# Attention stage of a four-layer kernel: division moved behind the values product, one subtraction moved to GpSimd

## What is computed

```python
ln = _ln(latents, g_l, b_l); xn = _ln(x, g_x, b_x)
q = ln @ w_q
k, v = jnp.split(jnp.concatenate([xn, ln], axis=1) @ w_kv, 2, axis=-1)
sim = jnp.einsum('bhid,bhjd->bhij', q * scale, k)       # masked keys: -max
attn = softmax(sim)
out = _ln(jnp.einsum('bhij,bhjd->bhid', attn, v) @ w_out, g_o, b_o)
x = x + jnp.tanh(g_xattn[0]) * out
```

## Time and profile before

| | us |
|---|---|
| median of 3 runs | 2226.71 |
| lowest, highest | 2226.37, 2227.58 |
| span of the profiled execution (no other time of it is recorded) | 2225.1 |
| TensorE busy in it | 2186.7 (98%) |
| weight loads | 1865.5 (84%) |
| VectorE | 1728.1 (78%) |
| ScalarE | 1282.0 (58%) |
| GpSimd | 645.1 (29%) |

### The profile page before, as it was taken

One profiled execution on the slowest core, in us unless ns is written; L12 is line 12 of the kernel. 1 busy time (PEld: TensorE's weight loads), 2 busy tenths in 40 slices (PEclk: granted clock), 3 DMA queues, 4 the chain that ended last, 5 costly groups with the idle time before them and its releaser, 6 DMA issues. The chain is left out here.

```text
span 2225.1 us, 48355 instructions
## 1 busy us (share of the span) xinstructions
PE 2186.7 (98%) x15486; PEld 1865.5 (84%) x15486; DVE 1728.1 (78%) x6112; ACT 1282.0 (58%) x3251; POOL 645.1 (29%) x1162
## 2 busy tenths in 40 slices
PE   8999999999999999999999999999999999999997
PEld 6777777777777777777699999999878888888886
DVE  6788888888888888888675555555579999999986
ACT  6776776776776776776443333433345555555553
POOL 1123223222232232232220000000355555555541
PEclk9999999999999999999899999999999999999999
DMA  5320110110110110110052222221212222222210
GB/s 189 124 97 22 37 40 23 37 39 21 40 38 20 39 39 20 40 32 27 11 161 73 81 86 72 81 77 41 89 58 65 65 65 64 65 65 65 65 39 20
DMA packets 111642, 129.57 MB, mean 58 GB/s; under 512 B 14898, under 2 KB 98089, under 8 KB 111264
## 3 DMA queue, kind: packets, MB, share of 16 engines
q1 hardware_dynamic: 98249, 105.06, 14.9%
q0 software_dynamic: 12288, 21.21, 3.3%
q10 hardware_dynamic: 855, 0.19, 0.0%
HBM read 84.26 MB, written 54.53 MB: 62 GB/s over the span
## 5 line engine op out<-in xcount | busy, mean ns | idle before, releaser
L711 ACT ACTIVATE a_prob<-a_prob,a_nmax 128x376 f32<-128x376 f32 x512 | 309.7, 606 | 155.3 <-DVE a_nmax L857 155.3
L1457 ACT ACTIVATE e_hidden<-e_first,keep_b 128x256 f32<-128x256 f32 x320 | 134.1, 471 | 283.3 <-PE e_first L80 282.8
L857 DVE CUSTOM_DVE_ANT_0 a_prob<-a_score,a_mask_row 128x376 f32<-128x376 f32 x512 | 266.6, 540 | 10.8 <-issue 5.6
L80 PE MATMUL e_second<-e_w,e_hidden 128*128 128x256 f32 x1920 | 239.5, 284 | 0.0
L80 PEld LDWEIGHTS e_second<-e_w,e_hidden 128*128 128x128 f32 x1920 | 232.6, 192 | 0.0
L869 DVE TENSOR_SCALAR a_prob<-a_prob,a_rden 128x376 f32<-128x376 f32 x512 | 220.9, 453 | 2.5
L1151 PE MATMUL a_turned<-keep_ident,a_prob 128*128 128x128 f32 (+1 forms) x1536 | 217.3, 277 | 2.8 <-DVE a_probT L876 1.6
L1151 PEld LDWEIGHTS a_turned<-keep_ident,a_prob 128*128 128x128 f32 (+1 forms) x1536 | 173.5, 142 | 43.5 <-issue 27.6
L1142 PE MATMUL a_score<-a_kT,a_qT 64*128 64x376 f32 x1024 | 196.4, 502 | 0.0
L876 DVE COPY a_probT<-a_turned 128x384 f32<-128x384 f32 x256 | 139.8, 546 | 54.4 <-PE a_turned L1151 54.4
L719 ACT ACTIVATE a_probT<-a_turned 128x384 f32<-128x384 f32 x256 | 124.9, 488 | 92.1 <-PE a_turned L1151 91.7
(11 more groups left out here) (237 smaller groups left out, 5231.1 us busy)
## 6 DMA issues: line engine op xcount, KB each, us to landing
w_in<-W SPq DMA_DIRECT2D x32, 512.0 KB, 4.1
slots<-a_zeros SPq DMA_DIRECT2D x8, 1280.0 KB, 8.7
keep_rows<-slots SPq DMA_DIRECT2D x40, 256.0 KB, 3.9
answers<-e_y SPq DMA_DIRECT2D x40, 256.0 KB, 2.2
a_xn<-x SPq DMA_DIRECT2D x32, 256.0 KB, 2.9
a_xr<-x SPq DMA_DIRECT2D x32, 256.0 KB, 3.8
x<-r_x SPq DMA_DIRECT2D x32, 256.0 KB, 4.0
w_in<-x SPq DMA_DIRECT2D x32, 256.0 KB, 2.6
```

The source lines that it names most:

```text
L80: last = nc.tensor.matmul(out, stationary(a, t), moving(b, t), start=start and n == 0, stop=stop and n == len(todo) - 1)
L711: nc.scalar.activation(prob[:, u % 4, a], prob[:, u % 4, a], ACT.Exp, bias=nmax[:, u % 4, a:a + 1], scale=-1.0, accum_out=den[:, u % 4, a: ...
L857: nc.vector.tensor_tensor_reduce(prob[:, u % 4, a], score[SCORE_AT[u][a]][:, 0:NKV], mask_row[:, p], -1.0, 3.0e38, ALU.add, ALU.min, nmax[ ...
L1457: nc.scalar.activation(hidden[:, 2 * j + i], first[:, j, i * CH:(i + 1) * CH], ACT.Relu, bias=b1[:, 2 * j + i, bass.ds(e, 1)]).then_inc(re ...
```

## The change

The rows stay undivided until after the values product. ScalarE's exponentials go straight to the turn, and the 256 x 64 result of each head is divided.

- `normalise` is gone; `turn_prob` waits for `exp_ok`.
- `over_sum(b, m)` is now once for each pair: a reciprocal of 128 x 4 sums (L905 in the new code), a wait for it on VectorE itself, and a turn in blocks of 32 x 32 (L908), so that a row holds the shares of 32 queries.
- SyncE's `spread_shares(b, m)` writes these rows to `shares` in HBM by four DMAs of 4 x 32 numbers (L580), waits until they have landed, and reads them back by two DMAs, each spread over 64 partitions (L584): `share[:, m]` has each query's share in every one of the head's 64 rows. The trips of m = 1, 2, 3 of s-2 stand after `store(s-4)`, that of m = 0 of s-1 after `load(s+2)` and ahead of the clears.
- VectorE's `attended` (L922) multiplies the bank by `share[:, m]` into `att` in SBUF, and with that the bank is free: TensorE's waits for a bank are on `att_ok` instead of `att_lo`.
- ScalarE's `att_high` now copies from `att`, and stands behind the copy of a turn where it stood ahead.
- `att_low` is on GpSimd (L643), from `att`. It stands first in GpSimd's step for pair 3 of s-3, behind the `zeroed` wait, and at three further places.

Core of the diff:

```diff
+            def spread_shares(b, m):
+                done = KI * b + m
+                eng.wait_ge(rden_ok, done + 1)
+                for g in range(0, P, 32):
+                    eng.dma_start(t["shares"][m, :, g:g + 32], rden_rows[g:g + 2 * QT, m % 2]).then_inc(share_out, 16)
+                eng.wait_ge(share_out, 64 * (done + 1))
+                at_least(eng, att_ok, done - KI + 1)
+                for a in range(2):
+                    eng.dma_start(share[64 * a:64 * a + 64, m],
+                                  t["shares"][m, QT * a:QT * (a + 1)].rearrange("i q -> (i q)").partition_broadcast(64)) \
+                        .then_inc(share_in[m], 16)
...
             def step(s, p):
...
                 if here(s - 4):
                     store(eng, s - 4, p)
+                if live(s - 2):
+                    spread_shares(s - 2, 1)
+                    spread_shares(s - 2, 2)
+                    spread_shares(s - 2, 3)
                 if live(s + 2):
                     load(s + 2, p)
+                if live(s - 1):
+                    spread_shares(s - 1, 0)
                 if isinstance(s, int) and s < N_CLEAR // 2:
                     clear_slots(2 * s)
                     clear_slots(2 * s + 1)
...
+            def att_low(b, m):
+                eng.wait_ge(att_hi, KI * b + m + 1)
+                nc.gpsimd.tensor_tensor(att2[:, 1, m], att[:, m], att2[:, 0, m].bitcast(F32),
+                                        ALU.subtract).then_inc(att_lo, 1)
...
                 if isinstance(s, int) and s == 4:
                     eng.wait_ge(zeroed, 16 * N_CLEAR)
+                if live(s - 3):
+                    att_low(s - 3, 3)
                 if here(s - 3):
                     norm1(eng, s - 3)
...
             def exps(b, u, a):
                 eng.wait_ge(nmax_ok[a], NG * b + u + 1)
+                at_least(eng, rden_ok, KI * b + u // 2 - 1)
...
             def att_high(b, m):
-                eng.wait_ge(pv_made, KI * b + m + 1)
+                eng.wait_ge(att_ok, KI * b + m + 1)
...
-            def over_sum(b, u):
+            def over_sum(b, m):
                 for a in range(2):
-                    eng.wait_ge(exp_ok[a], NG * b + u + 1)
-                nc.vector.reciprocal(rden[:, u % 4], den[:, u % 4]).then_inc(rden_ok, 1)
-            def normalise(b, u, a):
-                eng.wait_ge(rden_ok, NG * b + u + 1)
-                nc.vector.tensor_scalar(prob[:, u % 4, a], prob[:, u % 4, a], rden[:, u % 4, a:a + 1], None, ALU.mult) \
-                    .then_inc(norm_ok[a], 1)
+                    eng.wait_ge(exp_ok[a], NG * b + 2 * m + 2)
+                at_least(eng, share_out, 64 * (KI * b + m - 1))
...
+                nc.vector.reciprocal(rden[:, m % 2, 0:2 * QT].rearrange("p (a i) -> p i a", i=QT),
+                                     den[:, m % 2 * 2:m % 2 * 2 + 2]).then_inc(rden_made, 1)
+                eng.wait_ge(rden_made, KI * b + m + 1)
+                nc.vector.transpose(rden_rows[:, m % 2], rden[:, m % 2]).then_inc(rden_ok, 1)
...
+            def attended(b, m):
+                eng.wait_ge(pv_made, KI * b + m + 1)
+                eng.wait_ge(share_in[m], 32 * (b + 1))
+                at_least(eng, att_lo, KI * (b - 1) + m + 1)
+                nc.vector.tensor_tensor(att[:, m], (bank_a if m == 1 else bank_b)[:, 0:S], share[:, m],
+                                        ALU.mult).then_inc(att_ok, 1)
...
                 for a in range(2):
-                    eng.wait_ge(norm_ok[a], NG * b + u + 1)
+                    eng.wait_ge(exp_ok[a], NG * b + u + 1)
```

More of the change, by code:

```diff
@@ L469, in attend @@
             "k_made", "k_hi", "q_made", "q_hi", "v_made", "v_ok"))
[L470 to L474, removed]
+        mrow_ok, rden_set, rden_made, rden_ok, share_out = (
+            sem("a_" + s) for s in ("mrow_ok", "rden_set", "rden_made", "rden_ok", "share_out"))
+        share_in = [sem(f"a_share_in{m}") for m in range(KI)]
+        score_ok, nmax_ok, exp_ok, turned_ok, prob_ok = (
+            [sem(f"a_{s}{a}") for a in range(2)] for s in ("score_ok", "nmax_ok", "exp_ok", "turned_ok", "prob_ok"))
+        pv_made, att_ok, att_hi = (sem("a_" + s) for s in ("pv_made", "att_ok", "att_hi"))
         out_ok, stats1_ok = (sem("a_" + s) for s in ("out_ok", "stats1_ok"))
@@ L800, in step @@
                     turned_out(s - 2, 7, 0)
+                    att_high(s - 2, 2)
                 if live(s - 1):
@@ L928, in step @@
                     weights_lower(3, wo[:], stage_o)
-                if live(s - 2):
-                    normalise(s - 2, 2, 0)
                 if live(s - 3):
-                    att_low(s - 3, 3)
+                    attended(s - 3, 3)
                 if live(s - 2):
@@ L954, in step @@
                 if live(s - 2):
-                    normalise(s - 2, 3, 0)
+                    over_sum(s - 2, 1)
                 if here(s - 4):
                     choose(eng, s - 4, 4)
-                if live(s - 2):
-                    normalise(s - 2, 3, 1)
+                if live(s - 1) and not (isinstance(s, int) and s == 1):
+                    kvin_low(s - 1, q, 0)
                 if here(s - 4):
@@ L962, in step @@
                 if live(s - 1) and not (isinstance(s, int) and s == 1):
[L963 removed]
+                    kvin_low(s - 1, q, 1)
                 if here(s - 4):
                     choose(eng, s - 4, 6)
[L966 to L967 removed]
+                if live(s - 3):
+                    out_stat(s - 3)
                 if here(s - 4):
                     choose(eng, s - 4, 7)
[L970 to L971 removed]
                 if live(s - 2):
                     turned_out(s - 2, 2, 1)
+                if live(s - 3):
+                    out_centre(s - 3)
                 if routed(s - 4):
                     counts_in(eng, s - 4, bank_b)
[L976 to L977 removed]
                 if live(s - 2):
@@ L980, in step @@
                     row_max(s - 2, p, 6, 1)
-                    over_sum(s - 2, 4)
-                    normalise(s - 2, 4, 0)
-                    normalise(s - 2, 4, 1)
-                    att_low(s - 2, 0)
+                    over_sum(s - 2, 2)
+                    attended(s - 2, 0)
                     turned_out(s - 2, 3, 1)
@@ L1010, in step @@
                 if routed(s - 4):
+                    place(eng, s - 4, p, 1)
                     place(eng, s - 4, p, 2)
@@ L1016, in step @@
                 if live(s - 2):
-                    normalise(s - 2, 6, 1)
+                    attended(s - 2, 1)
                 if routed(s - 4):
@@ L1035, in step @@
                     row_max(s - 1, q, 2, 1)
-                    over_sum(s - 1, 0)
                 if live(s - 2):
-                    att_low(s - 2, 2)
+                    attended(s - 2, 2)
                 if here(s - 3):
```

83 lines of the change are left out of this document (32 added, 51 removed).

## The result

The changed kernel takes **2272.42 us** (median of 4 runs, 2272.18 to 2272.92), the kernel before 2227.14 beside it (4 runs, 2226.37 to 2229.88). The ratio is 1.0203, with a 95% interval from 1.0189 to 1.0217. It is slower, as forecast, but by 45 us where 9.8 were forecast, and outside the range that ended at 2245.

What follows compares the result with a forecast made beforehand. TensorE, busy without idle in the even steps, was taken as the bound. Stall 8.2, clock 2.3, first steps -1.4 and stage end +0.7 summed to 9.8 us on the median 2226.71, making 2236.5 us; range 2228 to 2245.

Steps and rivals of the forecast that it cites:

- The stall at the clears: Step 4: TensorE's output product waits for GpSimd's low part, held behind the late slot-table clears; 8.2 us.
- The clock: Behind the step 4 stall: TensorE's granted clock falls, slowing one output product; 2.3 us, bounds 1.31 and 4.6.
- First steps: Steps 2 and 3: TensorE's waits for divisions go or shrink; -1.4 us, between 0 and -2.1.
- End of the stage: Last output product of the first stage: GpSimd's low part and a hand-over join its wait; +0.7 us, between 0.4 and 1.4.
- Even steps, 0: First stage's even steps: TensorE waits for nobody and added work is covered, so the change costs 0 us.
- the tightest trip: Pair 3's reciprocals through SyncE's six DMAs in even steps: 7.9 us of 11.9 available, so covered.
- What VectorE is spared there is worth nothing: Even steps: removing 16 divisions of 0.45 us a step from VectorE gains nothing, as TensorE's work covers them.
- The first: Rival: clears in step 4 land by about 100.5 us despite the trip, no stall; 2226.0 us, 11%.
- second: Rival: 0.39 us of weight-load idle per step is a real wait for the division and goes; 2224.4 us, 8%.
- third: Rival: VectorE bounds the even steps, so removing divisions saves some 200 us; near 2030 us, 2%.
- The fourth: Rival: GpSimd's low part is late every step, each 0.1 us costing 2.9 us over 29 steps; 7%.
- The range: Forecast range for the whole kernel's time: 2228 (a small stall) to 2245 us (upper ends, some late low part).

Runs made afterwards that it cites:

- e2: Changed kernel with GpSimd's wait for the clears moved from the head of step 4 to just ahead of the first scatter; 2261.81 us.
- e10: Changed kernel with SyncE issuing the two clears ahead of the trip of pair 0's reciprocals, GpSimd's wait left in place; 2264.10 us.
- e6: Changed kernel with VectorE's last choice ahead of the statistics, counts ahead of the centring, and GpSimd's wait for the clears at the first scatter; 2231.17 us.
- e11: e6 with VectorE's split of the expert's weights moved, in the last step alone, behind the router's choice; 2230.86 us.
- e3: Changed kernel with VectorE's last choice ahead of the statistics and GpSimd's wait for the clears at the first scatter; 2248.73 us.
- e5: Changed kernel with VectorE's last choice ahead of the statistics and the counts read ahead of the centring; 2241.30 us.
- e9: Kernel before with its sixteen divisions a step left out; 2223.97 us.

## Why the prediction was wrong, point by point

- **The stall at the clears: right.** 8.31 us against 8.2. The clears were issued at 98.39 (98.85 forecast), the output product started at 108.59 (109.25). The trip's parts differed, and cancelled: the four writes were issued in 1.26 us, not 1.8, and the reads could follow at 96.54, not 97.95; the two reads took 1.80 to issue, not 0.9:

```profile
94.40 1.26 SPq L580 DMA_DIRECT2D shares<-a_rden_rows  x4
96.54 1.80 SPq L584 DMA_DIRECT2D a_share<-shares  x2
```

The last clear landed 8.6 us after its issue, where 9.1 were taken. e2 and e10 show that the stall needs the wait's place and the trip's.

- **The clock: right in kind,** 1.8 us for one output product against 2.3; e2, without the gap, has the product at 3.02.
- **First steps: -0.9** against -1.4, between the bounds. The division's 0.96 us of step 2 went, of step 3's 1.18 us 0.98 stayed, and 0.28 us at 37.75, for the copy of the values, are new:

```profile
64.68 1.67 PE L80 MATMUL a_work<-a_wkv,a_kvin 128*128 128x512 f32 x6 [0.98 <-DVE a_att L922]
```

- **End of the stage: +0.8** net against +0.7, but by other means, so the match is luck. The gap grew by 1.55, beyond the upper bound of 1.4, because the low part was priced at 0.65 alone and ran beside VectorE's split; a shorter output product gave half back. That product's time is not the change's: with the same end of the stage it took 4.58 in after, 4.76 in e2 and 5.46 in e6. e11's gap, 0.82 above the one before, is what the low part makes without the split beside it.
- **Even steps, 0: the step that failed.** It said that TensorE waits for nobody in the even steps, that its instructions are the same after the change, and that no new wait arises there; the sign to look for was a pitch of 33.6 us. It came to 34.65. Removed and added instructions were priced, and the tightest trip and the low part had their margins worked out, and these held (in the even steps no trip is waited for, and the output product starts without a wait). But the change also moves instructions that it neither adds nor removes, and these were not looked at: `choose(7)` behind the statistics, `counts_in` behind the centring. (They stand in the whole diff, not in the core of it that is shown under the change.) Both margins could be read in the rows of before that stand under the result. The statistics start at 507.27 and take some 1.1 us with their sum, so `ohs` behind them ends near 508.5, and with the 0.15 us from its end to the count (149.30 to 149.45 in the changed kernel) the count comes near 508.65 instead of 507.72: about 0.9 late. Measured, the count came 0.91 us later behind its turn (1.56 against 0.65). The counts end at 508.96 and are needed at 509.33: 0.37 us of margin, against a centring of 0.87: 0.5 late; measured 0.48 (e3). Missing from the sum were 1.0 us in step 4 and 31.1 in the 29 steps behind it; 29 of these are the two orders' (after against e5), 2 are open.
- **"What VectorE is spared there is worth nothing": right,** by e9.
- **The rivals.** The first would have needed clears that land early; they didn't. The second and third fell by e9. The Trainium skill's rule beside the third (Perfetto Trace Analysis, Identifying the Most-Contended Engine), by which weight-load time would make VectorE the most contended engine here, is not borne out by this case: without the divisions (e9) VectorE was busy for 47 of 252 us less, and the pitch stayed. The fourth had the right arithmetic, 2.9 us for each 0.1 us a step, and the wrong engine: GpSimd's piece took 0.74, not 0.65, and was in time; VectorE's choice cost ten such tenths a step.
- **The range** took in the unknown costs of added instructions alone, and 2% were left for everything unnamed. The case that came lay there.

## What to carry to other kernels

When an engine is busy without a gap, as TensorE is here, what its neighbours are spared is worth nothing, and any instruction moved behind a wait on a neighbour can cost on every pass of the loop. So go through the moved instructions as through the added ones: for each, which instruction with a wait now stands ahead of it, who waits for its result, and how long before that it was ready in the old trace. Two new waits on one chain need not add, as here, so mending one of them alone can look like half a cause or like none; test each order in the old kernel by itself.

## What was not expected of the hardware

GpSimd's and VectorE's operations with two inputs stretched when they met. At the stage's end of the changed kernel GpSimd's low part (alone 0.72) started at 1148.57, during VectorE's split (1148.23 to 1149.44), and took 1.45; VectorE's next product (L277, elsewhere 0.17) started at 1149.36 and ended at 1150.05, with GpSimd's piece, which ended at 1150.02. With the split moved (e11) they took 0.72 and 0.17. The Trainium skill's page SBUF — State Buffer, section Who interferes with whom, states that a VectorE instruction with two inputs in SBUF, as these have, contends with a GpSimd instruction that reads SBUF, and calls the pair of ports that they share an exclusive lock. The rows agree nearly: had GpSimd done nothing before the split's end at 1149.44, its 0.72 would make an end at 1150.16; measured 1150.02.

The clock at the stage's end was not a fixed cost: it stood at 0.50 for 16 us in the kernel before, through the last output product, and was back at 1.00 from 1098 us on in e9, which was worth more than the divisions themselves. How long TensorE stood does not tell the two apart. In the changed kernel the gaps around the clock's fall were much as in e9 (0.34, 0.69, 0.32 and 2.12 us against 0.34, 0.94 and 2.12), and its clock was still at 0.50 up to 1150 us, 12 us behind the last of these gaps:

```profile
1146.00:1150.00 4.00, 1.52 (x8) 0.53 (x4) 2.35 (x5) 0.42 (x1) 1.65 (x2) 0.50 0.00 0
```

What brings it back is not shown by these runs.
